# Two exact blocks in the query projection, seeded into its PSUM bank, and a new order inside the slot of a decoder-layer kernel

## What is computed

```python
x = x + attn(layernorm(x))       # 32 query heads, 8 key/value heads of 128, causal, RoPE
x = x + matmul(fake_quant(layernorm(x)), fake_quant(ctx))   # ctx is (2, 1024, 1024)
x = x + einsum('bsi,oi->bso', layernorm(x), binarized(weight))
# in attn, every projection weight is dequantised by blocks of 128 rows:
w = (codes.astype(float32) - 8.0) * repeat(scales, 128, axis=0)
q = hidden @ dequant(q_codes, q_scales)
```

## Time and profile before

| | us |
|---|---|
| median of 3 runs | 1079.08 (1077.76 to 1079.2) |
| profiled execution | 1078.07 |
| its span (first to last instruction) | 1076.2 |
| TensorE busy in the span | 1034.3 (96%) |
| VectorE, GpSimd, ScalarE busy | 940.6 (87%), 785.6 (73%), 727.8 (68%) |

### The profile page before, as it was taken

One profiled execution on the slowest core, in us unless ns is written; L12 is line 12 of the kernel. 1 busy time (PEld: TensorE's weight loads), 2 busy tenths in 40 slices (PEclk: granted clock), 3 DMA queues, 4 the chain that ended last, 5 costly groups with the idle time before them and its releaser, 6 DMA issues.

```text
span 1076.2 us, 19074 instructions
## 1 busy us (share of the span) xinstructions
PE 1034.3 (96%) x5356; PEld 503.9 (47%) x5356; DVE 940.6 (87%) x1741; ACT 727.8 (68%) x1589; POOL 785.6 (73%) x849
## 2 busy tenths in 40 slices
PE   5999998999999999999999999999999998989998
PEld 3444443444544454445445545544544453444443
DVE  7988998799888889888988889999999999878863
ACT  5547757767888888788878877777776776453320
POOL 4678888888888888788878888988888898332100
PEclk9999999999999999999999999999999999989999
DMA  9774303778667766666676666777776766423443
GB/s 340 246 189 131 110 20 83 154 146 163 166 147 165 157 151 151 160 161 153 153 156 157 154 152 152 160 150 153 158 165 148 151 128 130 119 83 64 98 103 79
DMA packets 309827, 156.13 MB, mean 145 GB/s; under 512 B 257728, under 2 KB 270400, under 8 KB 309728
## 3 DMA queue, kind: packets, MB, share of 16 engines
q1 hardware_dynamic: 301952, 141.69, 56.8%
q10 hardware_dynamic: 7776, 13.37, 3.9%
HBM read 89.20 MB, written 4.19 MB: 87 GB/s over the span
## 4 chain that ended last, share of the span: by engine, by line
POOL 49%; PE 18%; issue 17%; DVE 11%; ACT 2%; DMA 1%; POOLq 0%; DVEq 0%; SPq 0%; ACTq 0%
POOL w_b L1650 14%; POOL prob L1643 13%; POOL swapped L1638 7%; POOL rot L1658 4%; PE proj_ps L1107 4%; POOL q_sb L1663 3%; DVE rot L2018 2%; POOL ctx_raw L1771 2%; PE proj_ps L1112 2%; PE score_ps L1078 2%; POOL w_b L1744 2%; DVE x_acc L2113 1%; POOL rot L1686 1%; PE proj_ps L743 1%; PE proj_ps L744 1%
## 5 line engine op out<-in xcount | busy, mean ns | idle before, releaser
L1650 POOL TENSOR_TENSOR w_b<-prob,w_b 128x896 f16<-128x896 f32 (+2 forms) x192 | 188.6, 997 | 40.9 <-ACT w_b L1327 40.7
L1643 POOL TENSOR_SCALAR prob<-prob,row_inv 128x512 f32<-128x512 f32 (+3 forms) x256 | 166.8, 663 | 66.5 <-DVE row_inv L2191 60.8
L1300 ACT ACTIVATE prob<-score_ps,neg_max 128x512 f32<-128x512 f32 (+3 forms) x256 | 132.9, 522 | 74.5 <-DVE neg_max L2089 53.1
L745 PE MATMUL side_ps<-hT,w_a 128*128 128x512 f16 x444 | 168.3, 379 | 0.0
L744 PE MATMUL side_ps<-hT,w_a 128*128 128x512 f16 x444 | 168.3, 379 | 0.0
L743 PE MATMUL side_ps<-hT,w_a 128*128 128x512 f16 x444 | 168.3, 379 | 0.0
L2113 DVE SCALAR_TENSOR_TENSOR x_acc<-out_ps,o_now,x_acc 128x1024 f32<-128x1024 f32 x120 | 153.1, 1276 | 0.0
L2113 DVE SCALAR_TENSOR_TENSOR x_acc<-proj_ps,o_now,x_acc 128x1024 f32<-128x1024 f32 x120 | 152.6, 1272 | 0.0
L949 PE MATMUL proj_ps<-work,w_b 128*128 128x512 f16 x496 | 127.3, 379 | 4.7 <-issue 2.4
L949 PE MATMUL out_ps<-work,w_b 128*128 128x512 f16 x496 | 127.3, 379 | 0.9 <-DVE x_acc L2113 0.8
L2089 DVE CUSTOM_DVE_ANT_0 score_ps<-score_ps,mask_b 128x512 f32<-128x512 f32 (+3 forms) x256 | 121.7, 495 | 3.2 <-PE score_ps L912 3.1
(11 more groups left out here) (271 smaller groups left out, 2224.7 us busy)
## 6 DMA issues: line engine op xcount, KB each, us to landing
stage_c<-in_codes_dram SPq DMA_DIRECT2D x72, 256.0 KB, 2.9
stage_o<-in_codes_dram SPq DMA_DIRECT2D x64, 256.0 KB, 2.9
stage_s<-in_scales_dram SPq DMA_DIRECT2D x64, 256.0 KB, 3.5
ctx_raw<-in_ctx_dram ACTq DMA_DIRECT2D x32, 256.0 KB, 3.0
work<-w_b SPq DMA_TRANSPOSE x261, 3.1
x_acc<-in_x_dram SPq DMA_DIRECT2D x8, 512.0 KB, 8.4
k_sb<-in_codes_dram SPq DMA_DIRECT2D x16, 256.0 KB, 6.9
v_sb<-in_scales_dram SPq DMA_DIRECT2D x16, 256.0 KB, 7.3
```

What stands on the lines that cost most here:

```text
L745: return pe.matmul(o, stat(1), mov(0), start=False, stop=last)
L1300: ins = act.activation(prob[:, SCORE_AT[qb]:SCORE_AT[qb] + w], score_ps[:, score_bank(i, u), off:off + w], ACT.Exp, bias=neg_max[:, c:c + ...
L1643: return pool.tensor_scalar(prob[:, at:at + w], prob[:, at:at + w], row_inv[:, col:col + 1], P_UP, ALU.mult, ALU.mult)
L1650: ins = pool.tensor_tensor(prob16[:, 1, to:to + w], prob[:, at:at + w], prob16[:, 0, to:to + w], ALU.subtract)
```

## The change

Q's blocks 0 and 1 are both taken from exact codes. `q_exact` is now called twice: block 0 into `q_ps` (Q's own bank) and block 1 into `pv_ps`, 2 products each. ScalarE's `q_base` scales block 0 into `q_sum_in`; the new `q_seed` on VectorE takes `pv_ps` times its scale plus `q_sum_in` and writes it into `q_ps`, and the 18 products of blocks 2 to 7 accumulate onto that. `q_join` goes; `q_copy` on ScalarE copies the finished bank to `q_sum_in` for GpSimd's cosine, and `q_swap` reads the bank. `piece_scale` and `piece_lo` leave out 256 instead of 128 columns of every other piece, and `piece` copies 256 columns of codes there. The tables of scales get one more column, filled once by three small instructions in the K stage.

The order inside a slot changes on all engines:
- TensorE: `scores(0)`, exact 0, `o_unit(p-1,3)`, exact 1, `scores(1)`, `o_unit(p,0)`, `scores(2)`, Q's blocks 2 to 7, `o_unit(p,1)`, `o_unit(p,2)`, `weigh(p-1)`.
- ScalarE: `q_base`, `prob_split(p-1,1)`, the ctx tile's DMA, `exps(0)`, `o_cut`, `exps(1)`, `exps(2)`, ctx scaling, `q_hi`, `q_cut`, `q_copy`, `q_swap`, `prob_split(p,0)`, `ao_part(p-1)`, the last two ctx steps.
- VectorE: `q_seed` after `maxima(0)`, then `maxima(1)` and `(2)`, `o_add(p-1,3)`, a reciprocal, `q_sum`, `piece_scale`, `o_add(p,0)`, a reciprocal, `piece_lo`, and `o_add(p,1)` and `(p,2)` at the end.
- GpSimd: `q_turn(p+2)` stands between `norm` and `prob_rest`, and no longer behind `sine(p+1)`.

```diff
@@ -56,8 +56,8 @@
 STREAM_FIRST = KV_STREAM + FIRST_PIECES
 NEXT_FROM = SLOTS // 2
 Q_AHEAD = 2
-EXACT = P
-EARLY = 2
+N_EXACT = 2
+EXACT = N_EXACT * P
 Q_LEAD = 3
...
@@ -109,7 +109,7 @@
 CB = D // P
 UNITS = CB // B
 O_LAG = 3
-V_SLOTS = [(0, 2, 3, 5, 7), (7, 7, 8, 10, 12), (12, 12, 13, 16, 16)]
+V_SLOTS = [(0, 2, 3, 5, 7), (7, 7, 8, 10, 12), (12, 12, 15, 16, 16)]
 O_BACK = UNITS * O_LAG
 N_UNITS = NH * CB
 RING = 2
...
@@ -814,22 +815,28 @@
             mm = pe.transpose(pv_ps[:, c * P:(c + 1) * P], scale_rows[:, c * P:(c + 1) * P], ident[:, :])
         mm.then_inc(rows_turned, 1)
-    def q_exact(g, i):
+    def q_exact(g, i, e):
         h = i // B
         p = g * SLOTS + i
         pe.wait_ge(piece_done, g * SLOTS + (2 * h + 2))
-        pe.wait_ge(ao_ready, p - 3)
+        if e:
+            pe.wait_ge(ao_ready, p - 3)
+        elif known(p) and p == FIRST_PIECES:
+            pe.wait_ge(q_summed, 3)
+        else:
+            pe.wait_ge(q_swapped, p)
+        w = (h % RING * KB + e) * P
         for l in range(2):
-            mm = pe.matmul(pv_ps, w_a[:, 0, h % RING * KB * P:(h % RING * KB + 1) * P],
-                           hT[:, l, 0, i % B * S:(i % B + 1) * S], start=l == 0, stop=l == 1)
-        mm.then_inc(q_exact_done, 1)
+            mm = pe.matmul((q_ps, pv_ps)[e], w_a[:, 0, w:w + P], hT[:, l, e, i % B * S:(i % B + 1) * S],
+                           start=l == 0, stop=l == 1)
+        mm.then_inc(q_exact_done[e], 1)
     def q_part(g, i, kbs):
         h, b = divmod(i, B)
         p = g * SLOTS + i
-        first = 1 if by_parts(p) else 0
+        first = N_EXACT if by_parts(p) else 0
         if known(p) and p < Q_AHEAD and kbs[0] % 4 == 0:
             pe.wait_ge(piece_done, kbs[0] // 4 + 1)
         elif kbs[0] == first:
@@ -839,13 +846,14 @@
                 pe.wait_ge(h_ready, 2 * TB)
             elif known(p) and p == 1:
                 pe.wait_ge(o_table_ready, 1)
-            elif known(p) and p <= FIRST_PIECES:
-                pe.wait_ge(q_summed, (1, 1, 3)[p - 2])
+            elif known(p) and p < FIRST_PIECES:
+                pe.wait_ge(q_summed, 1)
             else:
-                pe.wait_ge(q_joined, p - FIRST_PIECES)
+                pe.wait_ge(q_seeded, p - FIRST_PIECES + 1)
         for kb in kbs:
             mm = three_products(q_bank(p), lambda l: w_a[:, l, (h % RING * KB + kb) * P:(h % RING * KB + kb + 1) * P],
-                                lambda l: hT[:, l, kb, b * S:(b + 1) * S], kb == first, kb == KB - 1)
+                                lambda l: hT[:, l, kb, b * S:(b + 1) * S],
+                                kb == first and not by_parts(p), kb == KB - 1, by_parts(p))
         if kbs[-1] == KB - 1:
             mm.then_inc(q_done, 1)
@@ -921,7 +929,7 @@
         else:
             pe.wait_ge(ao_ready, p)
         if not (known(p) and (p == 0 or p >= N_SLOTS - FIRST_PIECES + 1)):
-            pe.wait_ge(q_based, p)
+            pe.wait_ge(q_seeded, p)
         order = [(0, 0, 0), (0, 0, 1)] + [(kb, l, m) for kb in range(1, TB) for l, m in ((0, 0), (0, 1), (1, 0))]
         for kb, l, m in order + [(0, 1, 0)]:
...
@@ -979,32 +987,29 @@
         scores(p, i, g, 0)
         if v_at:
             v_blocks(v_at[1], v_at[2])
+        parts = by_parts(p + Q_AHEAD)
+        if has_ahead and parts:
+            q_exact(*ahead, 0)
         if has_o and not (known(p) and p == O_LAG):
             o_unit(p - 1, prev[1], 3)
+        if has_ahead and parts:
+            q_exact(*ahead, 1)
         scores(p, i, g, 1)
         if v_at:
             v_blocks(v_at[2], v_at[3])
-        parts = by_parts(p + Q_AHEAD)
-        if has_ahead and parts:
-            q_part(*ahead, range(1, EARLY))
         if has_o:
             o_unit(p, i, 0)
-        if has_ahead and parts:
-            q_exact(*ahead)
-        elif has_ahead:
+        if has_ahead and not parts:
             q_part(*ahead, range(0, 1))
-        if has_ahead and parts:
-            q_part(*ahead, range(EARLY, 3))
         scores(p, i, g, 2)
         if has_ahead and not parts:
             q_part(*ahead, range(1, 3))
         if v_at:
             v_blocks(v_at[3], v_at[4])
+        if has_ahead:
+            q_part(*ahead, range(N_EXACT if parts else 3, KB))
         if has_o:
             o_unit(p, i, 1)
-        if has_ahead:
-            q_part(*ahead, range(3, KB))
-        if has_o:
             o_unit(p, i, 2)
         if has_prev:
             weigh(p - 1, prev[1], prev[0])
...
@@ -1265,21 +1270,24 @@
             act.wait_ge(k_summed, K_TILES - 1)
         elif not (known(p) and p < Q_AHEAD):
             act.wait_ge(q_summed, p)
-        if by_parts(p):
-            act.wait_ge(q_joined, p - FIRST_PIECES + 1)
-        swap(q_swap_of(p), q_sum_in if by_parts(p) else q_bank(p), q_swapped)
+        swap(q_swap_of(p), q_bank(p), q_swapped)
+
+    def q_copy(p):
+
+        act.wait_ge(q_done, p + 1)
+        act.activation(q_sum_in, q_bank(p), ACT.Copy).then_inc(q_copied, 1)
     def q_base(g, i):
         p = g * SLOTS + i
-        act.wait_ge(q_exact_done, p - FIRST_PIECES + 1)
+        act.wait_ge(q_exact_done[0], p - FIRST_PIECES + 1)
         if not (known(p) and p == FIRST_PIECES):
             act.wait_ge(q_cosed, p)
         if known(p) and p < Q_LEAD * B:
             act.wait_ge(o_table_ready, 2)
         else:
             act.wait_ge(o_now_ready, g * RF + (i // B - (Q_LEAD - 1)))
-        act.activation(q_sum_in, pv_ps, ACT.Copy, scale=o_now[:, (i // B + 1) % 2, CB:CB + 1])\
+        act.activation(q_sum_in, q_ps, ACT.Copy, scale=o_now[:, (i // B + 1) % 2, CB:CB + 1])\
             .then_inc(q_based, 1)
     def q_hi(p):
...
@@ -1375,6 +1383,10 @@
         has_ahead = not (known(p) and p >= N_SLOTS - Q_AHEAD)
         has_piece = not (known(p) and p + FIRST_PIECES >= N_CUT)
+        if has_ahead and by_parts(p + Q_AHEAD):
+            q_base(*((g, i + Q_AHEAD) if i < SLOTS - Q_AHEAD else (g + 1, i + Q_AHEAD - SLOTS)))
+        if has_prev:
+            prob_split(p - 1, 1)
         if with_ctx:
             q, dst = ctx_half(g, i)
@@ -1388,16 +1400,15 @@
         exps(p, i, 0)
         if has_next and not by_parts(p + 1):
             q_hi(p + 1)
+        o_cut(p, i)
         exps(p, i, 1)
-        if has_ahead and by_parts(p + Q_AHEAD):
-            q_base(*((g, i + Q_AHEAD) if i < SLOTS - Q_AHEAD else (g + 1, i + Q_AHEAD - SLOTS)))
         if known(p) and wf_late(p) is not None:
             wf_upper(wf_late(p))
+        exps(p, i, 2)
         if with_ctx:
             act.wait_ge(ctx_landed, q * 16 + 16)
             act.activation(ctx_raw[:, :], ctx_raw[:, :], ACT.Identity, scale=scal[:, 5:6],
                            bias=scal[:, 3:4]).then_inc(ctx_scaled, 1)
-        exps(p, i, 2)
         if has_next and by_parts(p + 1):
             q_hi(p + 1)
         if has_piece:
@@ -1406,24 +1417,24 @@
             v_evict(V_HERE + p - 1)
         if known(p) and wf_early(p) is not None:
             wf_sign(wf_early(p))
-        o_cut(p, i)
+        if has_ahead and by_parts(p + Q_AHEAD):
+            q_copy(p + Q_AHEAD)
+        if has_ahead:
+            q_swap(p + Q_AHEAD)
+        if has_prev and known(p) and p < O_LAG:
+            ao_part(p - 1, i - 1)
         prob_split(p, 0)
+        if known(p) and p == N_SLOTS - 1:
+            prob_split(p, 1)
+            column_part(0, 0)
+        if not (known(p) and p < O_LAG):
+            ao_part(p - 1, (i - 1) % SLOTS)
         if with_ctx:
             act.wait_ge(ctx_clipped, q + 1)
             act.activation(ctx_raw[:, :], ctx_raw[:, :], ACT.Copy, bias=ROUND).then_inc(ctx_rounded, 1)
-        if has_prev and not (known(p) and p == N_SLOTS - 1):
-            ao_part(p - 1, (i - 1) % SLOTS)
-        if has_ahead:
-            q_swap(p + Q_AHEAD)
-        if known(p) and p == N_SLOTS - 1:
-            prob_split(p, 1)
-            column_part(0, 0)
-            ao_part(p - 1, i - 1)
-            return
-        prob_split(p, 1)
-        if with_ctx:
             act.wait_ge(ctx_rounded, q + 1)
             act.activation(dst, ctx_raw[:, :], ACT.Copy, bias=-(ROUND + Q_MID)).then_inc(ctx_free, 1)
+
     def q_first(n):
         piece(n, n % 2, q_region(n), Q_UP, (k_done, KB * K_ORDER.index((n // B * 2 + 1, 1)) + KB // 2 * (n % B + 1)))
...
@@ -1752,8 +1763,8 @@
                 q = (g - 1) * SLOTS + i
                 pool.wait_ge(ctx_free, q + 1)
             if not (known(p) and p >= N_SLOTS - 1) and by_parts(p + 1):
+                pool.wait_ge(q_ready, p + 1)
                 sine(swapped[:, :], q_swapped, p + 1, q_sined)
-                q_turn(p + 1)
             if known(p) and wf_early(p) is not None:
                 wf_clip(wf_early(p))
             if not (known(p) and p >= N_SLOTS - 1) and not by_parts(p + 1):
@@ -1774,6 +1785,8 @@
             pool.wait_ge(v_done, V_HERE)
             pool.wait_ge(inv_ready[1], p + 1)
             norm(1).then_inc(norm_done, 1)
```

(43 more changed lines are left out.)

31 lines of the change are left out of this document (17 added, 14 removed).

## The result

The changed kernel is slower. Its median is 1097.95 us (1097.06 to 1100.42, four runs) beside 1078.67 us for the kernel before on the same chip: a ratio of 1.0185 with a 95% interval of 1.0173 to 1.0197, some 19.3 us. The prediction was 1074.4 with a range up to 1084. The profiled execution has a span of 1095.2 us, 19.0 above that of before.

What follows compares the result with a forecast made beforehand. TensorE was taken to set the pace in the loop, VectorE from slot 40 on and in slots 3 to 7. Terms -5.2 + 0.5 + 0.3 - 0.5 + 0.2 = -4.7 gave 1074.4 us; range 1064 to 1084.

Steps and rivals of the forecast that it cites:

- slots 40 to 61: Late slots: a round through VectorE (8.56) and TensorE (3.24) takes 11.80 us, now 11.79; +0.3 us in all.
- regular slots: 29 loop slots: 11.565 us each against 11.745, so -5.2 us.
- heads of turns: Three first slots of loop turns: exact 1 and all behind it wait for `ao_rest`, 12.97 us each, +0.5 for three.
- slots 0 to 7: Slots 3 to 7, with much the same load as late slots: 5 x -0.1 = -0.5 us.
- the table: K stage: the new column of scales costs three instructions, +0.2 us.
- the tail: The tail of 178 us stays as before.
- TensorE paces the loop: Loop: TensorE sets the pace, waiting only 0.02 to 0.11 us a slot, so a packed slot falls from 11.68 to 11.465.
- The stall at the third scores: Loop: ScalarE's chain to `exps(0)` is ready at T + 3.86 against TensorE's 3.88; stall taken as 0.1 us a slot.
- The copy in the loop: Loop: the result of `maxima(0)` is there by T + 2.75, also in slots with `o_scales`, ahead of `exps(0)` at 3.04.
- The DMA: ScalarE's ctx DMA in the chain to `exps(0)`: counted at zero, hidden by `q_base` and `prob_split`; in line 0.63 us.
- Rival C: ScalarE at the slot's head: ctx DMA issued in line ahead of `exps(0)`, +0.63 on the chain; +10.1, 1089.2 us; chance 0.14.
- The rivals: Saved products come back in full, 1062.4 (0.07); gains cancel, 1079.6 (0.17); slower through ScalarE's DMA, 1089.2 (0.14).

Runs made afterwards that it cites:

- before_less_product: Kernel before, with the third product of Q's block 1 left out in 60 slots and nothing else changed: 1075.99 us.
- scales_by_reduce: Changed kernel, with VectorE's copy of ten scales written as a reduction over an axis of length one: 1091.28 us.
- clip_one_column: Changed kernel, with GpSimd's clip of the ctx tile working on one column in place of 512: 1093.18 us.
- the last kernel: Changed kernel with scales by reduction, ctx rounding ahead of `ao_part`, and, only outside the loop, `q_lo` behind `norm(1)` and exact 1 behind `scores(1)`: 1068.93 us.

## Why the prediction was wrong, step by step

On the profiled execution the forecast missed by 23.7 us. Against the prediction's own terms that is 12.8 in slots 40 to 61, 7.3 in the loop (4.2 in regular slots, 3.1 at the heads of turns), 4.6 in slots 0 to 7, 1.1 for the table and -2.1 in the tail. The step that failed above all is the price of the round through VectorE and TensorE in slots 40 to 61: 11.80 forecast, 12.44 measured. Its durations were taken over from the old order, and in the new one `wf_lower` takes 1.26 us beside `q_lo` and the copy 0.86 beside `prob_rest(0)`.

**TensorE paces the loop.** Only half true. (54 times 0.216 is 11.66 and not 11.64, which changes nothing.) TensorE did lose only 0.02 to 0.11 a slot, but in the earlier trace rows the third scores' load is released by `exps(0)`, inside a packed stretch: two chains ended together, and a product saved ahead of that point is worth nothing until the other chain gets shorter. before_less_product shows it: without the product, the same slot and 0.21 more of waiting.

**The stall at the third scores, 0.1 a slot from ScalarE's chain.** The place was right, the size too small (the mean slot is 11.711, 0.25 above the packed 11.46), and the cause another. The chain itself was drawn well: in scales_by_reduce's slot 11, where nothing else holds it, `exps(0)` starts at T + 3.06 (forecast 3.04). Of its two terms that stood in no row, the wait of L1436 for its own engine is 0.13 (taken as 0.1), and TensorE's start behind `ao_rest` 0.15 (taken as 0.11). What was missing are two other things that `exps(0)` waits for. In slots with the copy it waits for `maxima(0)`, and they give back 0.29 when the copy is a reduction. In the others it waits for `prob_rest(0)` on GpSimd, which in slot 10 ends at T + 3.15; they give back 0.12 of 0.19 with clip_one_column. The text gave GpSimd 1 us to spare and never had the end of `prob_rest(0)` ahead of `exps(0)`. Without the copy's collision the mean is 11.56, which meets the forecast by accident. So the 29 slots gave -1.0 and not -5.2.

**The copy in the loop.** The prediction says that the result of `maxima(0)` is there by T + 2.75 "also in slots with `o_scales`". The copy's 1.20 us stands between `ao_rest` and `maxima(0)`, and that made the claim false: at 518.49, 2.56 after T, `maxima(0)` only starts.

**Slots 40 to 61.** The drawn loop was the right one, its price wrong. TensorE's part, from `ao_rest` to `maxima(2)`, was put at 3.24; it is 3.64 (809.69 to 813.33) in a slot with the copy, and 3.42 in the next one. VectorE's, from there to the next `ao_rest`, was put at 8.82 and, in a slot with an exact piece, 8.29; it is 9.05 (813.33 to 822.38) and 8.78. On the mean that is 3.53 + 8.91 = 12.44 in place of 3.24 + 8.56 = 11.80. VectorE's durations were carried over from the old order as if they belonged to the instructions: `wf_lower` is 0.6 above its old median and the copy 0.7 every other slot, of which 0.22 reaches TensorE's part; another 0.29 of the 9.05 is VectorE's wait for `ao_part`. Against that `q_sum` gives back 0.17, and `piece_lo` (876/1010/1483 ns in the late slots of before, 410/677/680 after) some 0.3 to 0.4 for the same width: the old order had its collisions at other instructions, and a good part of them was counted into the 8.56 without being seen. With `q_lo` moved the late slots take 259.88 / 22 = 11.81, beside the forecast 11.80; since `wf_difference` takes a part of the collision over there, that agreement too is partly luck. The step should have had the question which GpSimd instruction runs beside each of VectorE's in the new order. Also missing was that `wf_lower` late makes ScalarE's `wf_sign` late and all behind it; that is read from the timeline above and was not tested apart.

**Slots 0 to 7.** Forecast -0.5, measured +4.05. Half of it is the same cause: slots 4 to 7 took 12.44, 12.42, 12.47 and 12.42, the same as late ones, 2.1 us more than before, and 11.53, 11.46, 11.67 and 11.53 in the last kernel. The other half is slot 2, which went from 10.81 to 12.71. There TensorE waits 0.74 at the third scores and 0.65 for the first `q_seed`. No edit changed that: it is 12.65 in the last kernel too, and its cause stays open.

**Heads of loop turns.** Forecast 12.97, measured 13.91 to 14.07. The step counted VectorE's gap and its `ao_rest` only. What ends last there is ScalarE's gap, through `q_base` and `q_seed`, and the rounding step at the end of the turn makes it longer. With that step moved the heads are 12.65 to 12.88. Three heads cost 3.6 us more than before, and with the -1.0 of the regular slots they make the loop's +2.60.

**The table's new column.** Forecast +0.2, measured 1.34 ahead of slot 0. 1.13 of it is one VectorE instruction of three columns (L2062), which takes 161 ns the first time and 1131 the second. The timeline has its partner:

```profile
89.58 1.19 POOL L1702 TENSOR_TENSOR k_sb<-rot,k_sb 128x512 f16<-128x512 f32 x1 [1.29 <-ACT k_sb L1258]
89.66 1.13 DVE L2062 TENSOR_SCALAR work<-stage_o 128x3 f32<-128x3 f32 x1
```

It starts 0.08 after a GpSimd instruction with two SBUF inputs and ends with it. That looks like the same collision in a third place; no run tested it here.

**The tail.** Forecast as before, measured -2.1. Over the profiles of the changed kernel and of its variants, whose edits hardly touch it, the stretch behind slot 61 takes 175.6 to 177.8 us. So a difference of 2.1 says nothing.

**The parts that held.** The exact products went from 120 to 240 with 60 fewer of each of the others. The DMA is issued at 518.15, 0.32 ahead of the instruction it is written behind, so it is out of the chain. Rival C, which had the right sign, had the wrong mechanism. `q_seed` takes 0.75 (forecast 0.68), and TensorE waits for it only 0.7 us in all, nearly all of it in slot 2.

**The rivals.** All of them, and the forecast, priced waits and durations of before. None was "VectorE's instructions get longer", so no chance stood against it, and the range, with its upper end 14 below the result, had no room for it.

## What to carry to other kernels

The spread of one form of instruction in a trace is a warning: a copy that takes 155 ns in one stage and 637 in another may well have a partner, and a new order can move the collision. Before moving VectorE's or GpSimd's work, list for each VectorE instruction with two SBUF inputs, and each float32 copy from SBUF to SBUF, what GpSimd does at that moment. And an engine that is busy for 96% of the span is not thereby the pace: look whether another engine releases a load in the middle of a packed stretch, for then two chains end together, or leave one product out and see whether the slot gets shorter.

## What was not expected of the hardware

- A VectorE copy of 128x10 float32 takes 1.20 us beside GpSimd's TENSOR_TENSOR of 896 columns, and 0.15 as a TENSOR_REDUCE at the same place. 128x256 with two SBUF inputs takes 1.26 beside `q_lo` and 0.47 away from it. In each of these rows VectorE's end lies 0.03 to 0.29 behind GpSimd's.
- GpSimd seems to pay as well: its `norm` has a mean of 766 ns in the kernel after and 663 in the kernel before. Which VectorE instruction stands beside it was not tested.
- Across the back edge of a loop ScalarE issues nothing for 1.76 and 2.44 us in the two rows above. The Trainium skill (Perfetto Trace Analysis, "DVE / Act Engine Instruction") lets the sequencer run ahead of the engine, which the DMA at 518.15 agrees with inside a turn; whether the gap at its end is the jump's own cost or a fetch of instructions no run here tells.
